# Local attention on one core: value and output weights folded per head, softmax weights turned in 32x32 blocks on VectorE

## What is computed

```
qkv = shift_tokens(x) @ Wqkv                      # 16 heads of 64; Wqkv 128 x 3072
q, k = rotate(l2norm(q) * qs), rotate(l2norm(k) * ksc)
sim  = einsum('bhwie,bhwje->bhwij', bq, bk2) * 8  # windows of 32 queries, 64 keys
attn = softmax(where(mask, -max, sim), -1)
out  = einsum('bhwij,bhwje->bhwie', attn, bv2)    # weights times values
x    = out @ Wo + x                               # Wo 1024 x 128
x    = feed_forward(shift_tokens(x)) + x
```

## Time and profile before

| | us |
|---|---|
| median of 3 runs | 3498.2 (3496.53 to 3501.21) |
| the profiled execution, span | 3500.8 |
| PE busy | 3344.2 (96%) |
| ACT busy | 2702.7 (77%) |
| DVE busy | 2441.7 (70%) |
| POOL busy | 1445.3 (41%) |

### The profile page before, as it was taken

How to read it: one execution, slowest core, us unless ns; L and a number is a source line. 1 busy time by engine, 2 the same in 40 slices (tenths; PEclk the granted TensorE clock), 3 DMA queues, 4 the chain that set the end, 5 groups by cost and what they waited for, 6 DMA issues and landing times.

```text
span 3500.8 us, 152322 instructions
## 1 busy us (share of the span) xinstructions
PE 3344.2 (96%) x63036; PEld 2479.3 (71%) x63228; DVE 2441.7 (70%) x5141; ACT 2702.7 (77%) x9033; POOL 1445.3 (41%) x1276
## 2 busy tenths in 40 slices
PE   6789999999999999999999999999999999999997
PEld 4457777677777767777767777767767767777775
DVE  5667777667777767777767777767767767777774
ACT  5667787768778777878777887868778787878876
POOL 2244444434444443444444444444444353444441
PEclk9899999999999999999999999999999999999998
DMA  2055656555655656565565566555555655565563
GB/s 71 1 115 122 140 122 129 121 123 120 143 123 123 132 118 134 127 130 126 112 138 118 127 135 131 120 130 117 127 129 121 133 129 127 117 130 126 116 135 76
DMA packets 361273, 421.42 MB, mean 120 GB/s; under 512 B 52291, under 2 KB 265814, under 8 KB 359814
## 3 DMA queue, kind: packets, MB, share of 16 engines
q1 hardware_dynamic: 360582, 411.67, 54.4%
HBM read 19.30 MB, written 2.10 MB: 6 GB/s over the span
## 4 chain that ended last, share of the span: by engine, by line
PE 69%; POOL 18%; issue 4%; DVE 2%; DMA 1%; ACT 1%; SPq 0%; POOLq 0%; DVEq 0%
PE ring_ps L1229 16%; POOL qs L612 12%; PE out_ps L1321 12%; PE out_ps L1331 9%; PE ring_ps L1274 8%; PE small_ps L1240 6%; PE score_ps L1292 4%; PE ring_ps L1303 4%; PE ring_ps L1367 4%; POOL probs L597 3%; DVE prod L988 2%; PE ring_ps L1264 2%; PE out_ps L1345 2%; PE score_ps L1284 1%; PE small_ps L1248 1%
## 5 line engine op out<-in xcount | busy, mean ns | idle before, releaser
L769 ACT ACTIVATE probs<-score_ps,neg_max,rq 128x64 f32<-128x64 f32 x3072 | 1194.7, 420 | 97.0 <-DVE neg_max L1026 95.7
L988 DVE TENSOR_TENSOR prod<-ring_ps,tables 128x512 f32<-128x512 f32 x1536 | 957.9, 681 | 292.4 <-PE ring_ps L1229 264.8
L612 POOL TENSOR_TENSOR ks<-prod 128x1024 f32<-128x1024 f32 x192 | 452.9, 2359 | 870.9 <-DVE prod L988 870.9
L1229 PE MATMUL ring_ps<-xs,wqk 128*128 128x256 f32 x3072 | 771.2, 389 | 17.2 <-issue 11.9
L769 ACT ACTIVATION_READ_ACCUMULATOR probs<-score_ps,neg_max,rq 128x1 f32 x3072 | 677.4, 221 | 0.0
L725 ACT ACTIVATE square<-ring_ps,biases 128x512 f32<-128x512 f32 x768 | 516.9, 687 | 200.9 <-DVE prod L988 199.1
L597 POOL TENSOR_TENSOR probs<-probs,inv_sums 128x512 f32<-128x512 f32 x384 | 401.0, 1044 | 608.8 <-DVE inv_sums L1040 608.7
L1229 PEld LDWEIGHTS ring_ps<-xs,wqk 128*128 128x128 f32 x3072 | 572.9, 192 | 107.3 <-issue 18.9
L612 POOL TENSOR_TENSOR qs<-prod 128x1024 f32<-128x1024 f32 x192 | 453.4, 2361 | 395.1 <-DVE prod L988 395.1
L1321 PEld LDWEIGHTS out_ps<-pt,v 64*64 64x64 f32 x24576 | 399.5, 136 | 119.2 <-issue 117.0
L758 ACT ACTIVATE att_t<-out_ps 128x512 f32<-128x512 f32 x384 | 217.0, 591 | 312.1 <-PE out_ps L1321 311.5
(11 more groups left out here) (182 smaller groups left out, 3809.4 us busy)
## 6 DMA issues: line engine op xcount, KB each, us to landing
v<-vs SPq DMA_DIRECT2D x1344, 128.0 KB
qt<-qs SPq DMA_DIRECT2D x768, 128.0 KB
kt<-ks SPq DMA_DIRECT2D x768, 128.0 KB
v<-vs SPq DMA_DIRECT2D x192, 64.0 KB
wqk<-in_L_ffn_Wqkv SPq DMA_DIRECT2D x6, 1024.0 KB, 5.2
wv<-in_L_ffn_Wqkv SPq DMA_DIRECT2D x6, 512.0 KB, 4.5
wo<-in_L_ffn_Wo SPq DMA_DIRECT2D x6, 512.0 KB
out_dram<-ks SPq DMA_DIRECT2D x16, 128.0 KB, 1.9
```

Source lines behind the costliest of these rows:

```text
L612: pool.tensor_tensor(dst, prod_a[p % 2], prod_b[p % 2], ALU.add).then_inc(rot_ready, 1)
L769: last = nc.scalar.activation(probs[i][:, j, e, :], score_ps[e][:, KEYS * j:KEYS * (j + 1)], ACT.Exp, bias=neg_max[:, h:h + 1], scale=rq[p ...
L988: last = V.tensor_tensor((prod_b if a else prod_a)[p % 2][:, f, :] .rearrange("p (u c) -> p u c", u=2), bank[:, :].rearrange("p (u c) -> p ...
L1229: last = mm(bank_of(s)[:, TOKENS * f:TOKENS * (f + 1)], wqk[:, n, 2 * c + f, a, :], xs[:, WINDOW:PADDED], start=True, stop=True)
```

## The change

The values are no longer made. For each head the product of its value weights and its output weights, 128x128, is made on the chip once per layer (`MF`, 4 steps, with the copies `MC` on ACT; `w_vo`). The softmax weights are turned by DVE in blocks of 32x32 (`TR` i,c, one 128x512 instruction each) and multiplied with x itself: `XT` (PE) turns x by four transpositions, `XC` (ACT) copies it, and `Y` i (PE) does 8 matmuls of 32 rows and 512 columns for a tile, each window in a row tile and a bank of its own. `OC` i,w (four on ACT, four on DVE) copy the eight banks into `y`, and `WO` sums 16 matmuls of 256 columns over the heads. `V`, `VC`, `MV`, `T`, `TC` and `PV` go. The ring has four banks and takes in `XT`, `UP`, `MF` and `Y`; the former `out_ps` are one bank, `fin_ps`. The order strings are new and carry for each step how many batches ahead it is. Computed is the same output.

```diff
 PE_ORDER = """
-PA0 PB0 PA1 S00 S01 PB1 BI WO PA2 NK CEN PB2 VAR PA3 PB3 TK UP0 UP1 S10 S11 V0 UP2 T00 TU NQ KN0 PAD V1 PV00 KN1
-TQ T01 V2 DN T10 PV01 V3 T11 PV10 PV11
+S00 S01 PA0:1 PB1:1 PA1:1 PB0:1 BI:-1 MF0:-1 MF1:-1 MF2:-1 MF3:-1 WO:-1 PA2:1 PB3:1 CEN:-1 PB2:1 NK:1 VAR:-1
+PA3:1 TK:1 S10 S11 XT:1 UP0:-1 UP1:-1 UP2:-1 TU:1 KN0:1 NQ:1 KN1:1 DN:-1 Y0 TQ:1 Y1
...
 DVE_ORDER = """
-XS RA0 RB0 RA1 M0 RB1 BI XA XB AR00 RA2 RB2 CK XG RB3 RA3 H0 M1 AR01 H1 TC00 UC H2 KM0 CQ VC1 KM1 AR10 TC01 X
-AR11 TC10 VC3 TC11
+OC13:-1 M0 RA0:1 RB1:1 RB0:1 RA1:1 AR00 BI:-1 XA:-1 XB:-1 RA2:1 TR00 RB2:1 CK:1 RB3:1 RA3:1 XG:-1 AR01 M1 UC:1
+H0:-1 H1:-1 H2:-1 KM0:1 KM1:1 TR01 CQ:1 X:-1 AR10 TR10 AR11 OC01 OC03 TR11 OC11 XS:2
...
 ACT_ORDER = """
-QA0 QB0 QA1 E00 QB1 E01 E02 SQ QA2 LN E03 QB2 RTK LG G0 QB3 QA3 G1 VC0 G2 LE E10 E11 E12 E13 VC2 OC00 OC01 OC10
-RTQ OC11
+E00 QA1:1 QA0:1 E01 QB0:1 QB1:1 E02 MC0:-1 MC1:-1 MC2:-1 MC3:-1 SQ:-1 E03 QA2:1 LN:-1 RTK:1 QB2:1 QB3:1 LG:-1
+QA3:1 G0:-1 XC:1 G1:-1 G2:-1 LE:-1 E10 E11 E12 E13 OC00 OC02 OC10 RTQ:1 OC12
...
 POOL_ORDER = """
-AD0 AD1 AD2 AN00 AD3 TB RK AN01 AN10 AN11
+AD0:1 AD1:1 AN00 AD2:1 AD3:1 TB:1 RK:1 AN01 AN10 AN11
...
 SP_ORDER = """
-LK MQ MK LV LL MV
+MQ:1 LK:1 MK:1 LV LL
...
-RING = [s for s in PE_ORDER if s[0] in ("PA", "PB", "TU", "KN", "V", "T", "DN", "PAD")]
-BANKS = 3
...
+RING = []
+for s_, ahead_ in PE_ORDER:
+    if s_[0] == "Y":
+        RING += [((*s_, w), ahead_) for w in range(WPT)]
+    elif s_[0] in ("PA", "PB", "TU", "KN", "XT", "UP", "DN", "MF", "PAD"):
+        RING.append((s_, ahead_))
+BANKS = 4
 assert len(RING) % BANKS == 0
+ACT_OUT, DVE_OUT = (of_kind(order, "OC") for order in (ACT_ORDER, DVE_ORDER))
+PROJECTIONS = of_kind(PE_ORDER, "PA", "PB")
+PRODUCTS = of_kind(DVE_ORDER, "RA", "RB")
+MF_BATCH = 12
...
+def folds(g):
+
+    if g == 0:
+        return 0
+    return g // BATCH + 1 if g % BATCH == MF_BATCH and g // BATCH < DEPTH - 1 else None
...
-                    act.wait_ge(prod_ready, at(g, QK_BANKS, rank(DVE_ORDER, ("RB" if a else "RA", p), "RA", "RB") + 1))
+                    act.wait_ge(prod_ready, at(g, QK_BANKS, PRODUCTS.index(("RB" if a else "RA", p)) + 1))
...
+                if kind == "XC":
+                    act.wait_ge(xt_made, at(g, 1, 1))
+                    if g >= 2:
+                        act.wait_ge(y_made, at(g - 1, TILES))
+                    nc.scalar.activation(xt[:, parity, :, :, :].rearrange("p t e c -> p (t e c)"), bank_of(("XT",))[:, :],
+                                         ACT.Copy).then_inc(xt_ready, 1)
...
                 if kind == "OC":
-                    i, c = s[1], s[2]
-                    act.wait_ge(pv_ready, at(g, TILES, i + 1))
-                    if i == 0 and c == 0:
+                    i, w = s[1], s[2]
+                    act.wait_ge(y_made, at(g, TILES, i + 1))
+                    if s == ACT_OUT[0]:
                         act.wait_ge(wo_ready, at(g, 1))
-                    nc.scalar.activation(att_t[:, :, P * i:P * (i + 1)].rearrange("p (j a) q -> p a j q", a=2)[:, c, :, :],
-                                         out_ps[c][:, :].rearrange("p (j c) -> p j c", c=P), ACT.Copy
-                                         ).then_inc(o_copied, 1)
+                    q0 = P * i + WINDOW * w
+                    nc.scalar.activation(y[:, :, q0:q0 + WINDOW], bank_of(("Y", i, w))[:, :].rearrange("p (h q) -> p h q", q=WINDOW),
+                                         ACT.Copy).then_inc(y_act_ready, 1)
...
-                if kind == "TC":
+                if kind == "TR":
                     i, c = s[1], s[2]
-                    dve.wait_ge(t_made, at(g, 2 * TILES, 2 * i + c + 1))
-                    dve.wait_ge(pv_ready, at(g, TILES, i))
-                    V.tensor_copy(pt[:, 4 * c:4 * c + 4, :], bank_of(("T", i, c))[:, :].rearrange("p (j c) -> p j c", c=P)
-                                  ).then_inc(t_copied, 1)
+                    dve.wait_ge(scaled, at(g, 2 * TILES, 2 * i + c + 1))
+                    if g >= 1:
+                        dve.wait_ge(y_made, at(g - 1, TILES, i + 1))
+                    V.transpose(pt[:, i, :, 8 * c:8 * c + 8, :],
+                                probs[i][:, 4 * c:4 * c + 4, :, :].rearrange("p j e (f k) -> p f (j e) k", f=2)
+                                ).then_inc(p_turned, 1)
+                if kind == "OC":
+                    i, w = s[1], s[2]
+                    dve.wait_ge(y_made, at(g, TILES, i + 1))
+                    if s == DVE_OUT[0]:
+                        dve.wait_ge(wo_ready, at(g, 1))
+                    q0 = P * i + WINDOW * w
+                    V.tensor_copy(y[:, :, q0:q0 + WINDOW], bank_of(("Y", i, w))[:, :].rearrange("p (h q) -> p h q", q=WINDOW)
+                                  ).then_inc(y_dve_ready, 1)
...
+                if kind == "XT":
+                    pe.wait_ge(xs_ready, at(g, 1, 1))
                     bank_free(g, s)
...
+                    for i in range(TILES):
+                        for half in range(2):
+                            last = pe.transpose(bank_of(s)[:, DIM * (2 * i + half):DIM * (2 * i + half + 1)],
+                                                xs[:, P * i + WINDOW * half:P * (i + 1) + WINDOW * half], ident[:, :])
+                    last.then_inc(xt_made, 1)
+                if kind == "MF" and folds(g) is not None:
...
+                    bank_free(g, s)
+                    rows = slice(DIM_HEAD * (c // 2), DIM_HEAD * (c // 2 + 1))
+                    for k in range(4):
+                        j = 4 * (c % 2) + k
+                        last = mm(bank_of(s)[:, DIM * k:DIM * (k + 1)], wv_t2[rows, j, :], wo[rows, j, :],
+                                  start=True, stop=True)
+                    last.then_inc(folded, 1)
...
+                if kind == "Y":
+
+                    i = s[1]
+                    if i == 0:
+                        pe.wait_ge(xt_ready, at(g, 1, 1))
+                    for w in range(WPT):
+                        bank_free(g, (*s, w))
+                    pe.wait_ge(p_turned, at(g, 2 * TILES, 2 * i + 2))
+                    for half in range(2):
                         for w in range(WPT):
...
+                            rows = slice(WINDOW * w, WINDOW * (w + 1))
+                            last = mm(bank_of((*s, w))[:, :], xt[rows, parity, i, half, :],
+                                      pt[rows, i, half, :, :].rearrange("p h q -> p (h q)"),
+                                      start=(half == 0), stop=(half == 1))
+                    last.then_inc(y_made, 1)
                 if kind == "WO":
 
-                    pe.wait_ge(o_copied, at(g, 2 * TILES, 2 * TILES))
-                    for j in range(PAIRS):
-                        last = mm(out_ps[0][:, 0:TOKENS], wo[layer % 2][:, j, :], att_t[:, j, :], start=(j == 0),
-                                  stop=(j == PAIRS - 1))
+                    pe.wait_ge(y_act_ready, at(g, len(ACT_OUT), len(ACT_OUT)))
+                    if DVE_OUT:
+                        pe.wait_ge(y_dve_ready, at(g, len(DVE_OUT), len(DVE_OUT)))
+                    if b == 0:
+                        pe.wait_ge(w_vo_ready, CREDIT + PARTS * (layer + 1))
+                        pe.wait_ge(b1_kept, 2 * (layer + 1))
+                    pe.wait_ge(log_ready, at(g, 1))
+                    for h in range(HEADS):
+                        last = mm(fin_ps[:, 0:TOKENS], w_vo[layer % 2][:, h, :], y[:, h, :], start=(h == 0),
+                                  stop=(h == HEADS - 1))
                     last.then_inc(wo_ready, 1)
...
                 if kind == "CEN":
-                    pe.wait_ge(xs1_ready, at(g, 1, 1))
-                    mm(out_ps[1][:, 0:TOKENS], center[:, :], xs1[:, :], start=True, stop=True).then_inc(cen_ready, 1)
+                    pe.wait_ge(xg_ready, at(g, 1))
+                    pe.wait_ge(x1_ready, at(g, 1, 1))
+                    mm(fin_ps[:, TOKENS:2 * TOKENS], center[:, :], xs1[:, :], start=True, stop=True).then_inc(cen_ready, 1)
```

304 lines of the change are left out of this document (132 added, 172 removed).

## The result

The changed kernel takes 3991.9 us (median of 4 runs, 3986.97 to 3993.58); the kernel before, beside it, 3497.4 (4 runs). The ratio is 1.141, with a 95% interval of 1.140 to 1.143. The profiled execution spans 3988.8 us. The forecast was 3750 us in a range of 3590 to 3900: right in its sign and in that loops of waits take PE's place, too low by 242 us.

What follows compares the result with a forecast made beforehand. Loop B, waits through PE and DVE, was to replace PE as the bound: 35.4 us a batch against 32.95, 235 us over 96 batches, plus 25 for foldings, on 3500.8 gives 3761; put at 3750 us, range 3590 to 3900.

Steps and rivals of the forecast that it cites:

- PE's sum, -1.5 us a batch: PE's own work per batch: 10.0 us removed, `WO`, `XT`, `Y` and foldings added, in all -1.5 us.
- Row tiles one after another: Rival, chance 0.05: `Y`'s row tiles don't overlap, 6.9 us a step, +9.5 us a batch, 4660 us in all.
- DVE's transposition at 0.65 us: Each `TR` on DVE was taken to cost 0.65 us, nearest to a copy.
- The dear transposition: Rival, chance 0.12: `TR` on DVE costs 1.3 us, lengthening loop B by 3 x 0.65: +190 us, 3940 us.
- The longer loop, 35.4 us: Loop B, the longer of two walked loops, takes PE's place: 35.4 us a batch, +2.45 against 32.95.
- loop A: Loop through ACT: `M` 0, products, squares, exponentials, last sums, `Y` 1, scores and copies, back to `M` 0: 35.0 us.
- loop B: Loop through PE and DVE: scores, projections, `WO`, products, `KM`, `X`, `Y` 0, `TR` 1,1, `Y` 1: 35.4 us.
- The half us of waiting in it becomes the wait for `CEN`: In loop A's 22.3 us from `QA` 1 to `E` 1,3, half a us of waiting becomes ACT's wait for `CEN`.
- Layer boundaries and slower stretches, which I keep as they are: The 1.1 us a batch by which the mean period exceeds the undisturbed 32.95 us, kept unchanged.
- Foldings, 4.2 us each, 25 in all: `MF` on PE: 32 records, 4.2 us, six times in the run, 25 us, paid in full ahead of `WO`.
- The rule on copies out of PSUM: By this rule alone PE stands 1.0 us a batch before the second `Y`: period 32.5 us, time near 3458.
- PE still sets the pace: Rival, chance 0.05: PE's own work, 31.5 us a batch, sets the period, 96 x 1.5 us gained, about 3360.

Runs made afterwards that it cites:

- experiment 3: Changed kernel with eight matmuls a batch that nobody reads put into PE's waits, three ahead of `Y` 0 and five ahead of `Y` 1: 3889.7 us.
- Experiment 5: Kernel of experiment 3 with ACT's exponentials `E` 0,1 moved ahead of the first squares: 3866.3 us.
- experiment 6: Kernel of experiment 3 with the first `Y` step (tile 0) halved, 4 of its 8 matmuls: 3894.7 us.
- experiment 1: Changed kernel with the next layer's Q/K weights and scales (`LK`) issued ahead of the rotated Q's moves (`MQ`): 3958.6 us.
- experiment 2: Changed kernel with DVE's bias sums of a new layer (`BI`) ahead of `AR` 0,0 instead of behind it: 3969.8 us.
- experiment 10: Kernel of experiment 3 with the same instructions in other orders on the engines, no step added or removed: 3710.1 us.
- experiment 12: Changed kernel with five filling matmuls ahead of `Y` 1 alone, none ahead of `Y` 0: 3903.1 us.
- experiment 4: Changed kernel without the foldings and their loads in layers 1 to 5, all layers using layer 0's folded weights: 3930.2 us.
- experiment 11: Like experiment 10's kernel, each `Y` step in two halves of eight heads, a few steps elsewhere, one and three filling matmuls: 3667.6 us.

## Why the prediction was right, and where it was wrong

- *PE's sum, -1.5 us a batch, and that it no longer counts.* Right. In experiment 3 PE's busy time without the filling matmuls is 3189 us (3556.4 - 367.0) against 3344.2 before, -1.6 a batch. In the changed kernel PE is busy 83%, and the two waits before `Y` (131 and 217 us in all) have the releasers that were named. `Y` at 2.15 us came out at 2.00 for 16 records, `WO` at 6.9 as put. One after another at 0.43 us a record it would be 6.9 us, so the row tiles run 3.4 at once; the rival *Row tiles one after another* is out.
- *DVE's transposition at 0.65 us.* 0.63 start to start, 0.71 by itself. The dear transposition is out, and with it the estimate of 1.24 us from the Trainium skill's "VectorE: DVE Perf Modes", section "The three transpose paths": the trace has 0.71 for 512 columns of four bytes.
- *The longer loop, 35.4 us.* Right in size (35.64), wrong in its path. Experiment 5 halves loop A's wait and experiment 6 shortens loop B's first `Y`; neither changes the ordinary period. The step of the path that failed is in loop A's walk, "The half us of waiting in it becomes the wait for `CEN`": that wait is the joint where ACT hangs on PE's output products, and the loop runs through it. The walks shared many steps with it, and the size came out within 0.24 us all the same; that close a hit, by a path that does not bind, is luck.
- *"Layer boundaries and slower stretches, which I keep as they are."* This is the step that carried the time out of the range. I kept 1.1 x 96 = 106 us; after the change they are 235 (93 + 50 + 92). The periods before the change, taken over 32.95 us in the same way, show what the 106 us were: 50 across layers' ends, 8 two after, 45 in the other 80, 2 in the five of batch 12. The change itself swaps `LK` and `MQ` and puts `BI` behind `AR` 0,0 in the very strings that I walked for the ordinary period; I did not walk them for the last batch of a layer. Experiments 1, 2 and 10 show that most of the 93 and 50 us is due to the order (12.5 us are left in experiment 10). And the 92 us are a cost that the forecast had no term for: with PE no longer full, its clock falls in the second `Y`. I had the idle stretches ("some 1.8 us before either `Y`") and put no price on them (experiments 3 and 12).
- *Foldings, 4.2 us each, 25 in all.* Counted as PE's records at full clock. The place of `MF` on the ring makes it wait for the squares (4.1 us), and `MF` itself and the first part of `WO` run at the low clock: 15 us over 35.64; without the foldings 1 us (experiment 4).
- *The sum.* Forecast for the profiled execution: 3761. Between the first and the last `XB`, +20 for the period (95 x 35.64 against 95 x 32.95 + 235), +129 for ends, stretches and clock, +51 for foldings (76 for five against 25 for six); outside, +27 (292 against 265: the first `XB` comes at 267.2 instead of 241.3. The first folding lies ahead of it, but most of this is order too: in experiment 10, with the same folding, it comes at 247.1). 3988, the span.
- *The rule on copies out of PSUM* ("TensorEngine Tiling (Array Packing)", section "PSUM Bottleneck", of the Trainium skill), by which the copies may become the limit: beside it the forecast worked out that PE would stand 1.0 us a batch for them, 3458 us in all. In the changed kernel PE waits before `Y` for the turned weights and for `x_all`; its weight loads for `Y` wait for the copies 12 us in all. The trace bears the rule out only once `Y` is split: then they wait 44 us.
- *PE still sets the pace* (3360 us). Out; even the best periods of experiment 11 stand at 35.0 us against 31.5 by the forecast's sum for PE alone.

What stays open: whether the loop can be brought under the 33 us of before, and how near the next limit is: with a shorter second `Y` the keys' moves come late more and more often (9, 31 and 62 places), and earlier keys were not tried. No version that I ran beats the kernel before.

## What to carry to other kernels

When an engine that was 96% busy is given less work, the pace passes to the loops of waits that its queue had covered; walk them to a joint, and price also the rare steps (a layer's end, a weight preparation) in the new order, since those hid beneath the full engine too. To learn which loop binds, shorten one step of each by a known amount and look at the period, not at the total: 35.64, 35.64, 34.78 and 36.24 told more than any busy share. And TensorE's idle time had a price of its own, paid by the matmuls behind it: 102 us here.

## What the runs showed of the hardware

- With TensorE idle for 1.41 and 2.26 us, the granted clock stood at 0.50 (1.2 GHz) in the 3 us after, and the 16 row-tile records there took 3.63 us instead of 2.00. Eight matmuls a batch that nobody reads, put into those stretches, gave back 102 us of 3992.
- It is not so in every period: 18 of the 78 ordinary ones escaped it, most of them with the same two waits. Where it comes, the low clock begins some 0.25 us later from one period to the next, until one escapes; what sets its place in the period no run here shows.
- Row tiles of 32 rows and 512 columns of float32: 16 records in 2.00 us with four tiles, 0.125 us each.
- DVE turns 128x512 float32 in blocks of 32x32 in 0.71 us, 0.63 from start to start, as a copy of that size (0.68 us by itself).
